# Normalising attention probabilities: 128x256 multiplications moved from GpSimd to ScalarE in a cross attention kernel

## The reference, cut to what matters

```python
xn = _layernorm(x, gamma, beta)                        # 64 batches of 32 queries
q = (xn @ w_q).reshape(B, SQ, NUM_HEADS, DIM_HEAD)     # 16 heads of 64
k, v = jnp.split(context @ w_kv, 2, axis=-1)           # context: 64 x 257 x 512
scores = jnp.einsum('bqhd,bkhd->bhqk', q * SCALE, k)
attn = jax.nn.softmax(scores, axis=-1)                 # over 257 keys
out = jnp.einsum('bhqk,bkhd->bqhd', attn, v).reshape(B, SQ, INNER)
out = (out @ w_out + b_out) * jnp.tanh(gate[0])
```

## Time and profile before

| | |
|---|---|
| three runs | median 1963.73 us, 1962.72 to 1965.52 |
| profiled execution | 1964.6 us, span 1962.8 us, mean granted TensorE clock 0.989 |
| TensorE busy | 1882.3 us, 96% |
| VectorE | 1045.7 us, 53% |
| ScalarE | 671.8 us, 34% |
| GpSimd | 557.3 us, 28% |

### The profile page before, as it was taken

How to read it: one execution, slowest core, us unless ns; L and a number is a source line. 1 busy time by engine, 2 the same in 40 slices (tenths; PEclk the granted TensorE clock), 3 DMA queues, 4 the chain that set the end, 5 groups by cost and what they waited for, 6 DMA issues and landing times. The chain is left out here.

```text
span 1962.8 us, 36613 instructions
## 1 busy us (share of the span) xinstructions
PE 1882.3 (96%) x14096; PEld 1613.8 (82%) x14096; DVE 1045.7 (53%) x2015; ACT 671.8 (34%) x1356; POOL 557.3 (28%) x546
## 2 busy tenths in 40 slices
PE   4989999999999999999999999599999999999999
PEld 3868888888988888898888889478877788888887
DVE  6624555455455545545554554468879963333322
ACT  2234444444444444444444444221111241111111
POOL 3015335434533543453354344331111100000000
PEclk9999999999999999999999999899999999999999
DMA  6323223222322322233232224623334040101010
GB/s 222 133 90 82 88 63 107 76 72 88 97 86 64 107 76 71 88 97 86 64 107 77 70 89 129 182 73 97 96 93 123 17 166 22 43 16 49 2 41 22
DMA packets 166581, 165.65 MB, mean 84 GB/s; under 512 B 8640, under 2 KB 123840, under 8 KB 166528
## 3 DMA queue, kind: packets, MB, share of 16 engines
q1 hardware_dynamic: 162096, 156.27, 26.3%
q10 hardware_dynamic: 4432, 8.65, 1.2%
HBM read 131.08 MB, written 33.82 MB: 84 GB/s over the span
## 5 line engine op out<-in xcount | busy, mean ns | idle before, releaser
L485 POOL TENSOR_TENSOR x_prob<-x_prob,x_share 128x256 f32<-128x256 f32 x256 | 157.5, 615 | 634.4 <-DVE x_share L652 627.3
L82 PE MATMUL x_ps<-w_cT_hi,w_space_hi 128*128 128x258 f32 x1024 | 299.8, 293 | 5.7 <-DVE w_space_lo L676 5.7
L83 PE MATMUL x_ps<-w_cT_lo,w_space_hi 128*128 128x258 f32 x1024 | 290.9, 284 | 0.0
L84 PE MATMUL x_ps<-w_cT_hi,w_space_lo 128*128 128x258 f32 x1024 | 289.3, 283 | 0.0
L676 DVE TENSOR_TENSOR w_space_lo<-x_ps,w_space_hi 128x512 fp32r<-128x512 f32 x256 | 164.6, 686 | 124.2 <-ACT w_space_hi L775 91.6
L669 DVE COPY x_mix<-x_ps 128x512 f32<-128x512 f32 x256 | 176.1, 688 | 85.4 <-PE x_ps L84 84.0
L82 PE MATMUL x_ps<-x_pT_hi,x_cn_hi 128*128 128x512 f32 x512 | 211.3, 413 | 1.5 <-DVE x_mix L669 1.5
L82 PEld LDWEIGHTS x_ps<-w_cT_hi,w_space_hi 128*128 128x128 f32 x1024 | 194.4, 190 | 12.7 <-DVE w_space_lo L676 8.8
L764 ACT ACTIVATE x_prob<-x_ps,x_negmax 128x257 f32<-128x257 f32 x256 | 121.9, 476 | 241.2 <-DVE x_negmax L647 241.2
L84 PE MATMUL x_ps<-x_pT_hi,x_cn_lo 128*128 128x512 f32 x512 | 201.4, 393 | 0.0
L83 PE MATMUL x_ps<-x_pT_lo,x_cn_hi 128*128 128x512 f32 x512 | 199.9, 390 | 0.0
(11 more groups left out here) (205 smaller groups left out, 3552.3 us busy)
## 6 DMA issues: line engine op xcount, KB each, us to landing
e_raw_T<-ctx_T SPq DMA_DIRECT2D x64, 514.0 KB, 4.0
e_raw_n<-ctx_nat SPq DMA_DIRECT2D x64, 512.0 KB, 3.6
q<-q_q ACTq DMA_DIRECT2D x16, 512.0 KB, 2.8
e_q<-q SPq DMA_DIRECT2D x16, 512.0 KB, 4.2
o_hi<-x_o_hi SPq DMA_DIRECT2D x32, 256.0 KB, 2.5
o_lo<-x_o_lo SPq DMA_DIRECT2D x32, 256.0 KB, 3.0
a_oT_hi<-o_hi SPq DMA_DIRECT2D x16, 512.0 KB, 4.4
a_oT_lo<-o_lo SPq DMA_DIRECT2D x16, 512.0 KB, 5.6
```

The source lines that it names most:

```text
L82: pe.matmul(out, lhs[0], rhs[0], start=start, stop=False)
L83: pe.matmul(out, lhs[0], rhs[1], start=False, stop=False)
L84: return pe.matmul(out, lhs[1], rhs[0], start=False, stop=stop)
L485: pool.tensor_tensor(prob[:, i, 0:KT * P], prob[:, i, 0:KT * P], share[:, i:i + 1].to_broadcast([P, KT * P]), ALU.mult)\
```

## The change

The four multiplications per batch leave GpSimd. ScalarE makes them as `activation` with the function Copy and `scale=share[:, i:i + 1]`, one scale per row, in place. In `softmax` the one of tile i - 1 stands right behind the exp of tile i, and that of the last tile at the end. At the end of a turn, where the order is written out, they stand as the diff shows. GpSimd keeps the last key's product and now waits for all four shares in one wait. The data, the counts and all other instructions stay as they are.

```diff
             def normalise(t, b):
-                for i in range(TILES):
-                    pool.wait_ge(share_done.sem, share_done.at(t, b * TILES + i + 1))
-                    pool.tensor_tensor(prob[:, i, 0:KT * P], prob[:, i, 0:KT * P],
-                                       share[:, i:i + 1].to_broadcast([P, KT * P]), ALU.mult)\
-                        .then_inc(probs_ready.sem, 1)
+                pool.wait_ge(share_done.sem, share_done.at(t, (b + 1) * TILES))
                 pool.tensor_tensor(last_z[:, :, b % GB], prob[:, :, SK - 1], share[:, :], ALU.mult)\
                     .then_inc(last_ready.sem, 1)
...
+            def normalise(t, b, i):
+                act.wait_ge(share_done.sem, share_done.at(t, b * TILES + i + 1))
+                act.activation(prob[:, i, 0:KT * P], prob[:, i, 0:KT * P], ACT.Copy, scale=share[:, i:i + 1])\
+                    .then_inc(probs_ready.sem, 1)
+
+            def softmax(t, b):
+                for i in range(TILES):
+                    exps(t, b, i)
+                    if i > 0:
+                        normalise(t, b, i - 1)
+                normalise(t, b, TILES - 1)
...
                     high_probs(t, b)
-                    for i in range(TILES):
-                        exps(t, b + 1, i)
+                    softmax(t, b + 1)
                     high_n(t, b + 1)
...
                     high_fold(t, 1, 6)
                     exps(t, GB, 0)
                     exps(t, GB, 1)
+                    normalise(t, GB, 0)
                     high_fold(t, 1, 7)
+                    normalise(t, GB, 1)
                     exps(t, GB, 2)
                     exps(t, GB, 3)
+                    normalise(t, GB, 2)
+                    normalise(t, GB, 3)
                     high_n(t, GB)
                     high_T(t, GB + 2)
...
-            for i in range(TILES):
-                exps(0, 0, i)
+            softmax(0, 0)
             high_n(0, 0)
```

## The result

The changed kernel takes 1967.5 us (median of 20 runs, 1965.2 to 1969.6), the kernel before 1963.8 (20 runs, 1962.2 to 1966.1). The ratio is 1.0018, with a 95% interval of 1.0011 to 1.0025: slower, by 3.7 us. It was forecast at 1967.0. The profiled execution took 1967.6, its span 1965.8 (before 1962.8). Of all the runs of all kernels here one stands apart, a run of e1_behind_fold7 that took 4786.7 us: it is in that kernel's median (1963.6 without it) and not in its interval.

The account below looks back on a forecast made before the run. TensorE was taken to bound the kernel. Fifteen delays of 0.23 us (3.4) less 0.1 in the prologue gave +3.3 us, so a median of 1967.0 us (+0.17%); range from 1963.6 less 0.3 to 1969.6.

Parts of the forecast that it names:

- The bound and the place: TensorE, busy 96%, bounds; fold 7, high_fold(7), low_fold(7), fourth score tile is a chain without slack once per turn.
- The size of the copy: Each new ScalarE normalise was to take 0.51 us and hold the engine for 0.40.
- the bounds: ScalarE's time per copy: lower bound 0.31 us, upper bound 0.56 with no overlap and a hand-over.
- The rival in which the operand is free: On ScalarE: a normalise holds it 0.31 us, high_fold(7) is 0.14 late, 1965.6 us; chance 0.13.
- The dearer copy: On ScalarE: a wait ends the overlap, normalise(0) holds 0.56 us, high_fold(7) is 0.39 late, 1969.6; chance 0.11.
- The sum: Fifteen turn ends at 0.23 us make 3.4, less 0.1 in the prologue: +3.3 us on the span.
- The prologue: First turn's transposes on TensorE wait less for GpSimd, tile 3 starting near 161.95: a gain of 0.1 us once.
- The covers: End of a softmax: high_n and low_n 0.80 us late, mix_chunk(3, 0) covered by 3.4, high_probs(3) 0.10 late: cost 0.
- the late load's rival: Softmax tail over 3.4 us late, so mix_chunk(3, 0) waits: 1983 us at one us beyond; chance 0.03.
- The faster rival: VectorE's work shortens with GpSimd quiet, the 0.38 us wait shrinks, at most 5.7 us, 1958.0; chance 0.06.
- Same or slower: Whole kernel: changes under 0.2% (3.9 us) count as same; chances same 0.66, slower 0.28, faster 0.06.

Follow-up runs that it names:

- e1_behind_fold7: Changed kernel with normalise(0) moved behind high_fold(7) instead of ahead of it at the end of a turn: 1963.8 us, ratio 0.9999.
- e2_end_on_gpsimd: Changed kernel with the four normalises at the end of a turn (60 of the 256) given back to GpSimd: 1964.0 us, ratio 1.0001.
- e4_constant_scale: Changed kernel with a constant as the scale of all 256 copies instead of the per-row share: 1965.6 us, ratio 1.0007.
- e7_middle_double: Changed kernel with a second copy behind each of the 196 normalises in mid-turn and prologue, none at a turn's end: 1968.6 us, ratio 1.0023.
- e5_before_hi_first: Kernel before, with TensorE's fourth tile doing its eight high-half products first and four low-half products last: 1954.7 us, ratio 0.9952.
- e8_double_hi_first: Changed kernel with a second copy between normalise(0) and high_fold(7), and the fourth tile's high-half products first: 1961.1 us, ratio 0.9989.
- e6_after_hi_first: Changed kernel with TensorE's fourth tile doing its high-half products first and its low-half products last: 1953.2 us, ratio 0.9948.

## Why the prediction was right, point by point

*The bound and the place.* TensorE's waits were the only thing to look at, and the one between fold 7 and the fourth tile was where the change met it. e1_behind_fold7 shows this by itself: one instruction moved by one place takes the whole cost away. e2_end_on_gpsimd shows the same from the other side.

*The size of the copy.* Forecast 0.51 us and a hold of 0.40; measured 0.499 and 0.40. The choice between the bounds, that a per-row operand costs what the exp's extra length shows, is confirmed by e4_constant_scale: 89 ns go with the operand. The Trainium skill's about 93 ns for each pointer operand ("ScalarE: Activation LUTs", section "What ACT_TABLE_LOAD costs") agrees with this. The rival in which the operand is free needed 1965.6 and a copy of 415 ns; both were seen, but only with a constant scale. The dearer copy is refuted by the same rows: it overlaps its neighbours though a wait stands ahead of it.

*The sum.* High_fold(7) was forecast 0.87 behind exp 1, and is. TensorE's wait was forecast at 9 us (0.61 each), and is 8.8 (0.59). 3.4 us were summed for the loop; TensorE's waits grew by 3.1 and the turns by 3.2, and the medians give 3.7 in all. The 0.5 us between the last two lie outside the turns, within the spread of the runs; the last tenths by which forecast and median agree are chance.

*The prologue.* A gain of 0.1 was forecast, tile 3 at 161.95 by the clock of the kernel before. TensorE there waited 1.0 us instead of 1.1: the right size, in one wait instead of two.

*The covers.* In the changed kernel the two normalises after exp 3 make high_n start 1.26 us behind that exp, 0.79 more than the earlier trace rows, where 0.80 was forecast. ScalarE after them, in the softmax of batch 3:

```profile
813.44 0.48 ACT L760 ACTIVATE x_prob<-x_ps,x_negmax 128x257 f32<-128x257 f32 x1 [0.49 <-DVE x_negmax L643]
...
813.90 0.90 ACT L765 ACTIVATE x_prob<-x_prob,x_share 128x256 f32<-128x256 f32 x2
814.70 1.04 ACT L754 ACTIVATE x_cn_hi<-e_raw_n 128x1024 fp32r<-128x1024 f32 x1
815.65 1.05 ACT L748 ACTIVATE w_cT_hi<-e_raw_T 128x1028 fp32r<-128x1028 f32 x1
816.60 1.06 ACT L778 ACTIVATE x_pT_hi<-x_ps 128x512 fp32r<-128x512 f32 x2
```

The idle of 0.60 ahead of high_probs(3) is used up, as forecast, and TensorE has no wait there. e7_middle_double doubled the lateness, and 2.65 us of cover were left; the late load's rival never came into play.

*The faster rival.* VectorE's low_fold(7) takes 1.29 us as before, with less on GpSimd, so the wait didn't shrink.

*Same or slower.* The forecast time was 0.6 us inside the bound of 0.2% and I called "no measurable change" the likeliest reading. By the ratio of 1.0018 the change is inside that bound, but the interval, 0.11% to 0.25%, lies across it: on which side the median fell was luck. 20 runs on each side put the whole interval above 1: it is a small loss, not none.

*What was sized wrong* lies outside the prediction's sum, in the experiments. I took the idle of 0.38 for the whole price of the stall, at most 5.7 us ("at most to nothing: 5.7 us, 1958.0" in the faster rival). Taking the stall away gave 9.3. The sum wasn't touched by this, since the new copy made a pause longer that was there already: the idle grew by 0.21 us a turn (0.38 to 0.59), and so did the turn.

## What to carry to other kernels

On an engine with a third of its time busy, 256 more instructions cost nothing in 241 places and everything in 15: look for the one place where the instruction ahead ends just as the bottleneck's data arrive, and put the new work behind, not ahead of it. Where a product is a sum of parts that need different inputs, do the parts first whose inputs are there first: this took more off than the moved multiplication had cost (9.3 against 3.7 us) and left it almost free in the same place, 0.4 us in 15 turns. The slack won is small, though: a second copy there cost its whole 0.40 us a turn again.

## What the runs showed of the hardware

- A per-row scale from memory made a ScalarE copy of 128x256 from SBUF 89 ns longer (499 against 410 ns) and held the engine 0.10 us longer (0.40 against 0.30).
- TensorE's idle time in the profile understated this stall. In the kernel before it gave 0.38 us a turn, but removing the stall brought the tile forward by 0.53 and made it 0.12 shorter: products of 258 columns are 0.12 us apart (three of them from 767.95 to 768.32 in e5_before_hi_first) but are each counted busy for 0.28, so that some 0.16 of the pause lies under the last one's length, and the tile that begins after a pause ran 1.64 us where it ran 1.52 without one (1.65 against 1.56 in e8_double_hi_first and e6_after_hi_first, with the same order of products). In the tile behind a pause the second product starts 0.22 us after the first (770.80 and 771.02 in e8_double_hi_first). 15 such turns make 9.8; the turns' lengths give 9.6, and 9.3 were measured.
